# Dense stage of a five-stage kernel: three layers in plain fp32 replaced by three fp32r products of parts, with ScalarE, VectorE and GpSimd making the parts

## The reference, cut to what matters

```python
o = o.reshape(b, n, n, D) @ W_out                 # 256 x 256
h = layer_norm(x + o, ln_agg_g, ln_agg_b)
m = jax.nn.relu(h @ W1 + b1) @ W2 + b2            # 256 -> 512 -> 256
t = layer_norm(m + h, ln2_g, ln2_b)
```

## Time and profile before

| what | value |
|---|---|
| median of 3 runs | 3976.84 us (3976.07 to 3978.92) |
| the profiled execution, its own time | 3975.38 us |
| its span, first to last instruction | 3973.6 us |
| mean granted TensorE clock, whole span | 0.972 |
| dense stage, first transpose to end of last `xT` | 1157.3 to 1501.2 us |

### The profile page before, as it was taken

How to read it: one execution, slowest core, us unless ns; L and a number is a source line. 1 busy time by engine, 2 the same in 40 slices (tenths; PEclk the granted TensorE clock), 3 DMA queues, 4 the chain that set the end, 5 groups by cost and what they waited for, 6 DMA issues and landing times. The chain is left out here.

```text
span 3973.6 us, 80632 instructions
## 1 busy us (share of the span) xinstructions
PE 3567.7 (90%) x30159; PEld 2955.0 (74%) x30159; DVE 2859.4 (72%) x4172; ACT 2435.9 (61%) x6243; POOL 1320.7 (33%) x740
## 2 busy tenths in 40 slices
PE   8977888788869997999999979999999979789887
PEld 5644555455548886888888878888888868688886
DVE  1558999899947774677777765777777766677787
ACT  3546888788845554566665655666666633677776
POOL 0008999899945542000000002000000013222254
PEclk9988999999989998999999989999999989999999
DMA  4573111311123323000000012000000046544565
GB/s 124 176 223 83 41 40 40 80 43 42 42 64 102 104 92 108 17 17 17 17 17 17 12 53 75 17 17 17 17 17 12 12 130 214 163 137 136 140 216 168
DMA packets 204751, 303.75 MB, mean 76 GB/s; under 512 B 18464, under 2 KB 156576, under 8 KB 201376
## 3 DMA queue, kind: packets, MB, share of 16 engines
q1 hardware_dynamic: 195232, 291.51, 24.3%
q10 hardware_dynamic: 9216, 8.39, 0.6%
HBM read 199.18 MB, written 100.66 MB: 75 GB/s over the span
## 5 line engine op out<-in xcount | busy, mean ns | idle before, releaser
L661 POOL TENSOR_TENSOR mx_big<-mp_lvs,mx_big 128x1280 f32<-128x1280 f32 (+1 forms) x256 | 802.0, 3213 | 327.0 <-ACT mp_lvs L587 312.5
L640 DVE TENSOR_TENSOR mx_big<-mp_psL,mx_big 128x2816 f32<-128x2816 f32 (+1 forms) x256 | 787.8, 3153 | 34.5 <-PE mp_psO L532 27.2
L594 ACT ACTIVATE mp_cut<-mp_psO,mx_mask 128x128 f32<-128x128 f32 x2048 | 550.7, 404 | 142.2 <-PE mp_psO L532 112.0
L532 PE MATMUL mp_psO<-mx_big,mp_pair 128*16 128x256 f32 x8192 | 499.6, 384 | 107.5 <-DVE mx_big L640 75.7
L1228 PE MATMUL sv_psO<-at_v_hi,sv_p_hi 128*128 128x258 f32 x2048 | 583.7, 285 | 13.1 <-DVE sv_p_lo L1316 10.1
L1228 PE MATMUL sv_psO<-at_v_lo,sv_p_hi 128*128 128x258 f32 x2048 | 578.5, 282 | 0.0
L1228 PE MATMUL sv_psO<-at_v_hi,sv_p_lo 128*128 128x258 f32 x2048 | 578.2, 282 | 0.0
L1247 ACT COPY sv_S<-sv_psS 128x512 f32<-128x512 f32 x512 | 300.5, 587 | 379.3 <-PE sv_psS L1202 274.4
L532 PEld LDWEIGHTS mp_psO<-mx_big,mp_pair 128*16 128x16 f32 x8192 | 326.1, 127 | 244.8 <-DVE mx_big L640 136.1
L1291 DVE TENSOR_TENSOR sv_run<-sv_run,sv_S 128x512 f32<-128x512 f32 x448 | 316.3, 706 | 249.1 <-ACT sv_S L1247 248.5
L1316 DVE TENSOR_TENSOR sv_p_lo<-sv_S,sv_p_hi 128x512 fp32r<-128x512 f32 x512 | 353.8, 691 | 107.6 <-ACT sv_p_hi L1256 107.2
(11 more groups left out here) (227 smaller groups left out, 7188.6 us busy)
## 6 DMA issues: line engine op xcount, KB each, us to landing
re_xg<-xg SPq DMA_DIRECT2D x192, 384.0 KB, 3.3
xg<-ga_xg SPq DMA_DIRECT2D x32, 768.0 KB, 3.9
att<-mx_big SPq DMA_DIRECT2D x16, 1024.0 KB, 5.5
mx_big<-rv SPq DMA_DIRECT2D x16, 1024.0 KB, 17.2
mp_pair<-att SPq DMA_DIRECT2D x128, 128.0 KB, 2.8
fr_xr<-in_x SPq DMA_DIRECT2D x16, 512.0 KB, 4.6
fr_xl<-in_x SPq DMA_DIRECT2D x32, 256.0 KB, 4.2
rv<-fr_rvs SPq DMA_DIRECT2D x16, 512.0 KB, 3.0
```

Of the source, the lines that this page charges most:

```text
L532: mm = pe.matmul(psO[32 * j:32 * j + 2 * H, c % 2, q, :], pair[:, s, :, :, c * YC + y], Z[:, c % 2, y, :], start=True, stop=True, tile_pos ...
L594: ins = nc.scalar.activation(cut[:, s, c, :, h * DK:(h + 1) * DK], psO[:, c % 2, :, h * DK:(h + 1) * DK], ACT.Copy, scale=mask[:, h:h + 1])
L640: nc.vector.tensor_tensor(Z[:, c % 2, 0:m], psL[:, s, 0:D].unsqueeze(1).broadcast_to([P, m, D]), big[:, rv_slot(b, c), 0:m], ALU.mult).the ...
L661: nc.gpsimd.tensor_tensor(Z[:, c % 2, m:YC], lvs[:, s, :].unsqueeze(1).broadcast_to([P, YC - m, D]), big[:, rv_slot(b, c), m:YC], ALU.mult ...
```

## The change

Each fp32 operand of the three layers is replaced by two fp32r parts: `hi`, the operand rounded to fp32r, and `lo`, the operand less `hi`, rounded to fp32r. A product of two operands becomes three products of parts, hi by hi, hi by lo, lo by hi, summed in the accumulator. So a tile has 60 fp32r products of 256 columns in place of 20 in fp32.

- Weights: before the rounds ScalarE copies `wo`, `wa`, `wb` to their `hi` parts, and VectorE subtracts for the `lo` parts.
- `oT`: ScalarE's copy writes `oT_hi`; VectorE subtracts it from `ps_o` into `oT_lo`.
- `hT`: ScalarE writes `hT_hi` with the gain alone; VectorE makes `hT_lo` with two operations of 256 columns. The bias that `hT` had is taken through `wa` once, by eight small products before the rounds, and added to `b1` (`b1s`).
- `mT`: ScalarE does each Relu twice, once into `mT_hi` and once into `mT` in fp32. GpSimd subtracts for the first two blocks of `mT_lo` and VectorE for the last two.
- `xoff` is made by two `tensor_scalar` operations in place of one `scalar_tensor_tensor`.
- Orders: TensorE now has turn `hn`(i-1), P1(i), turn `oin`(i+1), P3(i-2), turn `xl`(i-5), P2(i-1). ScalarE has `hT_hi`(i-1), T root(i-3), `oT_hi`(i+1), `xT`(i-5), H root(i), X root(i-4), Relus(i-1), `xl`(i-4). VectorE has `t0`(i-3), `mT_lo`(i-2), T moments(i-3), `hT_lo`(i-1), `tn`(i-3), `h0`(i), `oT_lo`(i+1), H moments(i), X moments(i-4), `hn`(i), `xoff`(i-4). GpSimd has `tg` and `ts` (i-3), `mT_lo`(i-1), `hg` and `hb` (i). SyncE's loads are issued for tile i+2 in round i, with the first two tiles ahead of the rounds.

```diff
@@ -685,17 +685,22 @@
...
+        wb_hi, wb_lo = (ph.sb(n, [P, MT, D], F32R) for n in ("wb_hi", "wb_lo"))
+        wo_hi, wo_lo = (ph.sb(n, [P, KT, D], F32R) for n in ("wo_hi", "wo_lo"))
+        wa_hi, wa_lo = (ph.sb(n, [P, KT, F1], F32R) for n in ("wa_hi", "wa_lo"))
...
+        b1s = ph.sb("b1s", [P, MT])
...
-        oT = ph.sb("oT", [P, 2, KT, W])
+        oT_hi, oT_lo = (ph.sb(n, [P, 2, KT, W], F32R) for n in ("oT_hi", "oT_lo"))
...
-        hT = ph.sb("hT", [P, 2, KT, W])
+        hT_hi, hT_lo = (ph.sb(n, [P, 2, KT, W], F32R) for n in ("hT_hi", "hT_lo"))
         mT = ph.sb("mT", [P, 2, MT, W])
+        mT_hi, mT_lo = (ph.sb(n, [P, 2, MT, W], F32R) for n in ("mT_hi", "mT_lo"))
...
@@ -758,13 +765,19 @@
...
+                def load(i):
+                    reach(sp, o_turned, i - 1)
+                    reach(sp, added1, i - 1)
+                    for c in range(2):
+                        sp.dma_start(oin[c * N:(c + 1) * N, i % 2], ox[i * U:(i + 1) * U, c].rearrange("u y d -> y u d")).then_inc(in_[i % 2], 16)
+                    sp.dma_start(xres[:, i % 2], tile_rows(x.rearrange("b x y d -> (b x y) d"), i)).then_inc(in_[i % 2], 16)
...
+                load(0)
+                load(1)
                 for i in range(LAST + 1):
-                    if i < NT:
-                        reach(sp, o_turned, i - 1)
-                        reach(sp, added1, i - 1)
-                        for c in range(2):
-                            sp.dma_start(oin[c * N:(c + 1) * N, i % 2], ox[i * U:(i + 1) * U, c].rearrange("u y d -> y u d")).then_inc(in_[i % 2], 16)
-                        sp.dma_start(xres[:, i % 2], tile_rows(x.rearrange("b x y d -> (b x y) d"), i)).then_inc(in_[i % 2], 16)
+                    if i + 2 < NT:
+                        load(i + 2)
...
@@ -785,47 +798,73 @@
...
+                def parts(k):
+
+                    return ((0, 0, k), (0, 1, k), (1, 0, k))
...
                 pe.wait_ge(w_in, 16 * len(loads))
+                for f in range(MT):
+                    for k in range(KT):
+                        mm = pe.matmul(ps_m[:, f, 0:1], wa[:, k, f * P:(f + 1) * P], b1nc[:, k:k + 1], start=(k == 0), stop=(k == KT - 1))
+                mm.then_inc(b1_turned, 1)
+
+                def turn_o(i):
+                    pe.wait_ge(in_[i % 2], (i // 2 + 1) * 48)
+                    reach(pe, oT_kept, i)
+                    turn(ps_o, oin[:, i % 2], o_turned)
+
+                turn_o(0)
                 for i in range(LAST + 1):
-                    if i < NT:
-                        pe.wait_ge(in_[i % 2], (i // 2 + 1) * 48)
-                        reach(pe, oT_kept, i)
-                        turn(ps_o, oin[:, i % 2], o_turned)
                     n = i - 1
                     if 0 <= n < NT:
                         pe.wait_ge(ln[H_LN]["normed"], n + 1)
                         reach(pe, hT_kept, n)
                         turn(ps_h, hn[:, n % 2], h_turned)
+                    if i < NT:
+                        pe.wait_ge(oT_kept, i + 1)
+                        reach(pe, added1, i)
+                        reach(pe, w_cut, 1)
+                        for u in range(U):
+                            terms = [t for k in range(KT) for t in parts(k)]
+                            for e, (a, c, k) in enumerate(terms):
+                                mm = pe.matmul(ps_1[:, u * D:(u + 1) * D], oTs[a][:, i % 2, k, u * P:(u + 1) * P], wos[c][:, k, :],
+                                               start=(e == 0), stop=(e == len(terms) - 1))
+                        mm.then_inc(made1, 1)
+                    if i + 1 < NT:
+                        turn_o(i + 1)
+                    n = i - 2
+                    if 0 <= n < NT:
+                        pe.wait_ge(mT_lo_pool, n + 1)
+                        pe.wait_ge(mT_lo_dve, n + 1)
+                        pe.wait_ge(w_cut, 3)
+                        reach(pe, added3, n)
+                        for u in range(U):
+                            terms = [t for k in range(MT) for t in parts(k)]
+                            for e, (a, c, k) in enumerate(terms):
+                                mm = pe.matmul(ps_3[:, u * D:(u + 1) * D], mTs[a][:, n % 2, k, u * P:(u + 1) * P], wbs[c][:, k, :],
+                                               start=(e == 0), stop=(e == len(terms) - 1))
+                        mm.then_inc(made3, 1)
                     n = i - 5
                     if 0 <= n < NT:
                         pe.wait_ge(ln[X_LN]["normed"], n + 1)
                         reach(pe, xT_kept, n)
                         turn(ps_x, xl[:, n % 2], x_turned)
-                    if i < NT:
-                        pe.wait_ge(oT_kept, i + 1)
-                        reach(pe, added1, i)
-                        by_token(ps_1, oT[:, i % 2], wo, KT, made1)
                     n = i - 1
                     if 0 <= n < NT:
                         pe.wait_ge(hT_kept, n + 1)
+                        pe.wait_ge(w_cut, 2)
+                        pe.wait_ge(b1_made, 1)
                         for f in range(MT):
                             if f % 2 == 0:
                                 reach(pe, mT_made, (n - 1) * 2 + f // 2 + 1)
-                            for k in range(KT):
-                                mm = pe.matmul(ps_m[:, f, :], wa[:, k, f * P:(f + 1) * P], hT[:, n % 2, k, :], start=(k == 0), stop=(k == KT - 1))
+                            terms = [t for k in range(KT) for t in parts(k)]
+                            for e, (a, c, k) in enumerate(terms):
+                                mm = pe.matmul(ps_m[:, f, :], was[c][:, k, f * P:(f + 1) * P], hTs[a][:, n % 2, k, :],
+                                               start=(e == 0), stop=(e == len(terms) - 1))
                             if f % 2 == 1:
                                 mm.then_inc(made2, 1)
-                    n = i - 2
-                    if 0 <= n < NT:
-                        pe.wait_ge(mT_made, n * 2 + 2)
-                        reach(pe, added3, n)
-                        by_token(ps_3, mT[:, n % 2], wb, MT, made3)
...
@@ -838,20 +877,28 @@
...
+                nc.scalar.copy(wo_hi[:, :, :], wo[:, :, :]).then_inc(w_hi_cut, 1)
+                nc.scalar.copy(wa_hi[:, :, :], wa[:, :, :]).then_inc(w_hi_cut, 1)
+                nc.scalar.copy(wb_hi[:, :, :], wb[:, :, :]).then_inc(w_hi_cut, 1)
+
+                def keep_oT_hi(i):
+                    act.wait_ge(o_turned, i + 1)
+                    reach(act, made1, i - 1)
+                    keep(oT_hi[:, i % 2], ps_o, oT_hi_kept)
+
+                keep_oT_hi(0)
                 for i in range(LAST + 1):
-                    if i < NT:
-                        act.wait_ge(o_turned, i + 1)
-                        keep(oT[:, i % 2], ps_o, oT_kept)
                     n = i - 1
                     if 0 <= n < NT:
                         act.wait_ge(h_turned, n + 1)
                         for k in range(KT):
-                            ins = nc.scalar.activation(hT[:, n % 2, k, :], ps_h[:, k * W:(k + 1) * W], ACT.Identity,
-                                                       bias=b1nc[:, k:k + 1], scale=g1c[:, k:k + 1])
-                        ins.then_inc(hT_kept, 1)
+                            ins = nc.scalar.activation(hT_hi[:, n % 2, k, :], ps_h[:, k * W:(k + 1) * W], ACT.Copy, scale=g1c[:, k:k + 1])
+                        ins.then_inc(hT_hi_kept, 1)
                     n = i - 3
                     if 0 <= n < NT:
                         root(T_LN, n)
+                    if i + 1 < NT:
+                        keep_oT_hi(i + 1)
...
@@ -864,10 +911,17 @@
...
                     n = i - 1
                     if 0 <= n < NT:
+                        act.wait_ge(b1_made, 1)
+                        reach(act, made3, n - 1)
+                        reach(act, mT_lo_pool, n - 1)
+                        reach(act, mT_lo_dve, n - 1)
                         for f in range(MT):
                             if f % 2 == 0:
                                 act.wait_ge(made2, n * 2 + f // 2 + 1)
-                            ins = nc.scalar.activation(mT[:, n % 2, f, :], ps_m[:, f, :], ACT.Relu, bias=b1c[:, f:f + 1])
+                            ins = nc.scalar.activation(mT_hi[:, n % 2, f, :], ps_m[:, f, :], ACT.Relu, bias=b1s[:, f:f + 1])
+                            if f % 2 == 1:
+                                ins.then_inc(mT_hi_made, 1)
+                            ins = nc.scalar.activation(mT[:, n % 2, f, :], ps_m[:, f, :], ACT.Relu, bias=b1s[:, f:f + 1])
                             if f % 2 == 1:
                                 ins.then_inc(mT_made, 1)
...
@@ -901,20 +955,53 @@
...
+                for j, (lo, full, hi) in enumerate(((wo_lo, wo, wo_hi), (wa_lo, wa, wa_hi), (wb_lo, wb, wb_hi))):
+                    dve.wait_ge(w_hi_cut, j + 1)
+                    nc.vector.tensor_tensor(lo[:, :, :], full[:, :, :], hi[:, :, :], ALU.subtract).then_inc(w_cut, 1)
```

(47 more changed lines are left out.)

9 lines of the change are left out of this document (3 added, 6 removed).

## The result

The changed kernel takes 3998.42 us (median of 4 runs, 3993.92 to 4003.08); beside it on the same chip the kernel before took 3976.45 (3975.59 to 3978.92). The ratio is 1.0061, 95% interval 1.0048 to 1.0074: slower by 22 us by the medians and 24 us by the ratio (19 to 29 by its interval). The profiled execution took 3993.92, its span is 3992.0, its mean granted clock 0.972.

What follows compares the result with a forecast made beforehand. TensorE was taken to bound the kernel at 10.01 us a round, afterwards a loop of waits at 10.64; +17.0, +3.7 and -3.0 gave +17.7 on 3975.4, or 3993.1, with 1.5 for the median 3994.6; range for all 3972 to 4008.

Steps and rivals of the forecast that it cites:

- The loop: Dense-stage round: Relus, VectorE's `mT_lo` held behind GpSimd's `hg`, T moments, `hT_lo`; 10.64 us against 10.01, 27 rounds +17.0.
- The first loop: Dense-stage round through VectorE's `hT_lo` to X moments, then ScalarE's X root, eight Relus, `xl`, `hT_hi`: 9.95 us.
- The first rival: VectorE gets the port first or misses GpSimd: round 9.95, 3974.5 us, no change; chance 0.18.
- the start: Dense stage up to the first X moment: weight copies, subtractions and early waits move it from 1199.68 to 1203.4, +3.7 us.
- the end: From tile 27's X moments to the last `xT`, 31.1 us before: earlier, shorter P3 and unwaiting `xoff` give -3.0.
- The rival with TensorE as the bound: `hT_hi` not in effect behind Relus and `xl`: round falls to TensorE's 8.5, 3935.3 us; chance 0.08.
- The cover of P2: TensorE in the round: P2's first half done at 14.7, its Relus at 15.6, so 0.9 us to spare.
- P3 comes earlier in its round, and shorter: TensorE's P3 at the dense stage's close: one reason given for saving 3 us there.
- the clock for the rounds: TensorE's clock falling through idle gaps in dense rounds: 27 x 4.6 = +125, 4102 us if throughout; chance 0.03.
- the sum: Dense-stage total: +17.0 for 27 rounds, +3.7 at its start, -3.0 at its end: +17.7 us.
- What was costed at nothing: Dense-round work taken as covered: P2's first half, `oT_hi`, T root, `oT_lo`, loads, `hb`, two `xoff` operations, `hT_hi` without bias.

## Why the prediction came out as it did

**The loop, right.** The round is set by Relus, a held `mT_lo`, T moments, `hT_lo` and back. Measured from 1305.51 to 1316.05, `hT_lo` to `hT_lo`, it takes 10.54, of which 4.99 to the first Relu, as predicted, and 5.55 from there, predicted 5.65. VectorE asked 0.17 after `hg` started (predicted 0.18), ended 0.55 behind it as before, and waited 1.41 for the Relus, where I took 1.2. What was too much is one term: the T moments and the step to `hT_lo` were put at 0.96 behind the end of `mT_lo`, and take 0.86, since they start 0.08 before that record ends. The round shown is 10.54; 27 rounds of 10.51 on average instead of 10.64 are +13.5, not +17.0.

**That it is this loop and no other** is shown by five runs. The hold is what counts: with `hg` out of the way the loss is gone (round 9.75), and with `hg` made to wait, 9.75 and the new hold on `tn`. The queue behind is what counts: with the hold kept and the T moments ahead of it, 9.88. The first loop did not set it (`hT_hi` before `xl`, 10.51), and neither did TensorE (a third of its products, 10.50). The first rival was therefore real, 0.17 us away: its 9.95 and 3974.5 came as 9.75 and 3976.89 once the order was changed. That the times agree so well is luck: the rounds gave 7 us, not 1.6, the start took 6 more than before, not 2.3, and the end gave nothing, not 3. The rival with TensorE as the bound gave 3935.3; no run reached it. With `xl` out of the first loop and the hold off `mT_lo` the round is 8.97, not 8.5, and the time 3958.29, and loops still set it.

**The cover of P2, rightly sized and used up later.** The prediction gave P2's first half 0.9 to spare ahead of its Relus. In the changed kernel it is 0.78. The prediction did not follow this path as a loop of its own; with the orders changed it became the one that sets the round (9.88 twice).

**The start, mis-sized.** The term was +3.7 and measured +5.0. I took 0.8 for the first P1; it starts at 1161.56 against 1159.19, 2.4 later. The prediction priced ScalarE's copies and VectorE's subtractions, and left out that TensorE now makes the products of the bias, sixteen records in 3.57 us, ahead of the first turn. They end at 1159.20, and the first turn (1159.06) stands right behind them, 1.7 later than before. About 1.0 of that is theirs; the last load of tile 0 also landed 0.7 later than before, at 1157.9. The other 0.7 up to P1 is `oT_lo`. From P1 to the first X moment it is 2.7 more than before, where the prediction has 2.9.

**The end, wrong in its sign.** -3.0 was predicted, +2.4 came. The step that failed is "P3 comes earlier in its round, and shorter". P3 does come earlier in TensorE's order, but without new tiles it stands and waits for `mT_lo`, 3.24 at 1493.83 and 2.54 at 1504.24, and P2 of the last tile, whose input was ready at 1495.4, stands behind the first of the two until 1498.60. Nor are they shorter. The granted clock is 1.00 from 1488 to 1493, 0.72 from 1493 to 1499, 1.00 from 1499 to 1504 and 0.66 from 1504 to 1509: it is low in both P3, after both waits. Their products start 0.21 apart at first, instead of 0.12, and they take 4.4 us each (to 1498.24 and to 1508.59) instead of the 2.95 of a P3 in the rounds. Both are in the chain that ends the stage, so this is 2.9 of the 5.4 by which the term is off. I had weighed the clock for the rounds, where it stayed at 1.00, and not for the end.

**The hand-over, not thought of,** cost 0.6: SyncE issues the next stage's first load 6.1 after the last `xT`, against 5.5. The changed kernel has nine more semaphores; whether that is the cause was not tried, and with the same semaphores the version with `hg` first took 7.2.

So +17.7 was forecast for the sum and +21.5 is what the dense stage shows. The misses, -3.5, +1.3, +5.4 and the 0.6 of the hand-over, partly cancel, and the 3.0 us that the other stages gave in this execution brought the profiled time (3993.9) closer to the forecast than the working deserves.

**What was costed at nothing** held for `hb` (drawn out to 1.61 by `mT_lo`, and nobody waits for it), for the loads and for the two `xoff` operations. `hT_hi` without a bias is not the same in length: two take 0.87 instead of 1.03. In this kernel that changes nothing, since VectorE is late by 0.85 anyway. What the Trainium skill (SBUF — State Buffer, section "Who interferes with whom") says of the pair of ports, that the first to start holds it for its whole instruction, was seen before on one side only; now both are shown, VectorE's 1.65 in `hg` and GpSimd's 1.74 in `mT_lo`.
